# Gate matmuls in token groups inside a norm stage, in a one-core GNN and MoE kernel

## What is computed

```python
x = x + _L0_gnn_ref(_layernorm(x, axis=-1), ...)        # GIN layer: gather, two matmuls with batch norm
x = x + _L0_ffn_ref(_layernorm(x, axis=-1)[None], gate_w, experts)[0]
x = x + _L1_gnn_ref(_layernorm(x, axis=-1), ...)        # weighted gather, one matmul
x = x + _L1_ffn_ref(_layernorm(x, axis=-1)[None], ...)[0]   # 8 leaves, 512 -> 2048 -> 512 each
```

```python
gates = jnp.einsum('bhnd,hde->bhne', x4, gate_w)        # 1250 x 512 times 512 x 8
t = jnp.log(jnp.clip(gates, EPS)) / TEMPERATURE
for 8 iterations:                                       # Sinkhorn
    t = t - logsumexp(t, axis=-2)                       # over tokens
    t = t - logsumexp(t, axis=-1)                       # over experts
vals, idx = top_k(exp(t) per expert, 1250 // 8)
gate_values = (vals > 0.5)
routed = xf[idx]; outputs = einsum('hmei,eio->hmeo', routed, experts) * gate_values
```

## Time and profile before

| | us |
|---|---|
| median of 3 runs | 2508.84 |
| lowest, highest | 2504.61, 2509.62 |
| the profiled execution | 2508.55 |
| span of its trace | 2506.8 |
| norm stage c, first transpose to last lo part | 401.32 to 428.07 |
| from there to the start of `plan` | 428.07 to 441.14 |
| Sinkhorn, thresholds and places | 441.14 to 495.82 |

### The profile page before, as it was taken

The page is one execution under the profiler, slowest core; times in us unless marked ns, Lnnn a source line. Parts: engine busy times, 40 slices in busy tenths (PEclk is TensorE's granted clock), DMA queues, the critical chain, the costliest instruction groups (busy, mean ns, idle before and its releaser), DMA issues. The chain is left out here.

```text
span 2506.8 us, 34028 instructions
## 1 busy us (share of the span) xinstructions
PE 2298.5 (92%) x13384; PEld 2224.4 (89%) x13384; DVE 1033.3 (41%) x1695; ACT 701.1 (28%) x1204; POOL 323.6 (13%) x310
## 2 busy tenths in 40 slices
PE   3888886387989999999999999999999999999996
PEld 3777886366869999999999999999999999999996
DVE  7993346536362424324242432424233242423422
ACT  1335223064232222222222222222222222222221
POOL 1452000012001011101101110111111011101101
PEclk9998997598989999999999999999999999999998
DMA  1000201151020102102010210201011020101001
GB/s 65 2 2 1 68 1 49 47 189 52 34 77 2 68 1 78 34 34 78 1 67 6 72 34 34 78 1 67 13 65 34 34 78 1 67 17 61 34 1 41
DMA packets 73339, 105.93 MB, mean 42 GB/s; under 512 B 7219, under 2 KB 42499, under 8 KB 73211
## 3 DMA queue, kind: packets, MB, share of 16 engines
q1 hardware_dynamic: 68731, 100.37, 11.6%
q0 software_dynamic: 4480, 3.64, 0.5%
HBM read 95.08 MB, written 10.40 MB: 42 GB/s over the span
## 5 line engine op out<-in xcount | busy, mean ns | idle before, releaser
L1528 DVE TENSOR_TENSOR hidden_lo<-gelu,hidden_hi 128x416 fp32r<-128x416 f32 (+1 forms) x384 | 247.8, 645 | 1133.6 <-ACT hidden_hi L1596 1133.6
L1592 ACT ACTIVATE gelu<-psum,b1cols 128x416 f32<-128x416 f32 (+1 forms) x384 | 233.8, 609 | 1234.6 <-PE psum L475 1234.5
L473 PE MATMUL psum<-f_xT_hi,w_hi 128*128 128x416 f32 (+1 forms) x1536 | 543.2, 354 | 0.2 <-ACTq L1584 0.2
L473 PE MATMUL psum<-hidden_hi,w_hi 128*128 128x416 f32 (+1 forms) x1536 | 541.8, 353 | 1.4 <-DVE leaf_factors L1554 1.4
L474 PE MATMUL psum<-f_xT_lo,w_hi 128*128 128x416 f32 (+1 forms) x1536 | 542.0, 353 | 0.0
L475 PE MATMUL psum<-hidden_hi,w_lo 128*128 128x416 f32 (+1 forms) x1536 | 541.7, 353 | 0.0
L475 PE MATMUL psum<-f_xT_hi,w_lo 128*128 128x416 f32 (+1 forms) x1536 | 541.5, 353 | 0.0
L474 PE MATMUL psum<-hidden_lo,w_hi 128*128 128x416 f32 (+1 forms) x1536 | 539.2, 351 | 0.0
L1575 POOL TENSOR_TENSOR acc<-acc,y_scaled 128x416 f32<-128x416 f32 (+1 forms) x192 | 198.9, 1068 | 1544.8 <-DVE y_scaled L1519 1544.8
L473 PEld LDWEIGHTS psum<-f_xT_hi,w_hi 128*128 128x128 f32 x1536 | 290.1, 189 | 4.8 <-issue 1.9
L475 PEld LDWEIGHTS psum<-f_xT_hi,w_lo 128*128 128x128 f32 x1536 | 290.1, 189 | 4.2
(11 more groups left out here) (275 smaller groups left out, 1992.3 us busy)
## 6 DMA issues: line engine op xcount, KB each, us to landing
w_raw<-in_w SPq DMA_DIRECT2D x128, 512.0 KB, 4.1
expert_raw<-in_experts SPq DMA_DIRECT2D x8, 1024.0 KB, 5.8
leaf_all<-leaf_rows SPq DMA_DIRECT2D x8, 625.0 KB, 3.7
rows_by_place_d<-zero_rows SPq DMA_DIRECT2D x1, 2560.0 KB, 15.9
rows_by_place<-rows_by_place_d SPq DMA_DIRECT2D x5, 512.0 KB, 7.7
expert_results_d<-expert_results SPq DMA_DIRECT2D x16, 160.0 KB, 4.9
x_rows<-in_x SPq DMA_DIRECT2D x1, 2500.0 KB
out_rows<-x_rows SPq DMA_DIRECT2D x10, 250.0 KB
```

The costliest lines, as they stand in the source:

```text
L473: t.matmul(out, stat[0], mov[0], start=start, stop=False)
L1528: v.tensor_tensor(hlo[:, s % 4, 0:w], G[:, s % 3, 0:w], hhi[:, s % 4, 0:w].bitcast(F32), ALU.subtract).then_inc(lo_cut, 1)
L1592: a.activation(G[:, s % 3, 0:w], g.psum[:, 4 + s % 4, 0:w], ACT.Gelu, bias=g.b1cols[:, bass.ds(e * 16 + half * 8 + 2 * q + j, 1)]).then_in ...
```

## The change

A function `add_norm_gate` takes the place of `add_norm_turn` for this stage, and the gate part leaves `phase_route`.

```diff
+def add_norm_gate(nc, sem, g, produce, rows, thi, tlo):
+    LAG = 3
+    GROUPS = [(0, 4), (4, 8), (8, NT)]
...
+    def cols(i):
+        return g.psum[:, 4 + i % 3, 0:KD * TR].rearrange("p (k c) -> p k c", k=KD)
...
+        @block.sync
+        def _(sp):
+            for e in range(2):
+                sp.dma_start(g.eraw[:, e], g.experts[e].rearrange("(k p) d -> p k d", p=128)).then_inc(
+                    g.w_loaded[e], 16)
...
+        @block.vector
...
+            s.mark(v.memset(ghi[:, :, :].bitcast(F32), 0.0))
+            s.mark(v.memset(glo[:, :, :].bitcast(F32), 0.0))
+            s.wait()
+            s.then(v.tensor_copy(ghi[:, :, 0:NE], g.gate[:, :, :]))
+            v.tensor_tensor(glo[:, :, 0:NE], g.gate[:, :, :], ghi[:, :, 0:NE].bitcast(F32),
+                            ALU.subtract).then_inc(gate_cut, 1)
...
+        @block.scalar
...
+                if i < NT:
+                    deviation(a, g, stats, i)
+                if i in (8, 12):
+                    copy_gates((i - 8) // 4)
+            copy_gates(2)
...
+        @block.tensor
+        def _(t):
+            def gates(n):
+                lo, hi = GROUPS[n][0] * TR, GROUPS[n][1] * TR
+                t.wait_ge(lo_cut, GROUPS[n][1])
+                if n:
+                    t.wait_ge(gates_copied, n)
+                else:
+                    t.wait_ge(gate_cut, 1)
+                for k in range(KD):
+                    ins = cut_products(t, g.psum[:, 3, 0:hi - lo], (ghi[:, k, :], glo[:, k, :]),
+                                       (thi[:, k, lo:hi], tlo[:, k, lo:hi]), k == 0, k == KD - 1)
+                ins.then_inc(gated, 1)
...
+            for i in range(NT + LAG):
+                if i < NT:
+                    if i >= 3:
+                        t.wait_ge(added, i - 2)
+                    produce(t, i, g.psum[0:TR, i % 3, :]).then_inc(produced, 1)
+                j = i - LAG
+                if j >= 0:
+                    t.wait_ge(normed, j + 1)
+                    if j >= 3:
+                        t.wait_ge(lo_cut, j - 2)
...
+                    ins.then_inc(turned, 1)
+                if i == 8:
+                    gates(0)
+                if i == 11:
+                    turn_gates(0)
+                    gates(1)
+            turn_gates(1)
+            gates(2)
+            turn_gates(2).then_inc(g.gates_turned, 1)
```

More of the change, by code:

```diff
@@ L46 @@
 CH = PLACES // 2
+GATE_BANK = 7
 NG = NP // 128
@@ L873, in phase_route @@
     room = Room(nc, g.route_at)
-    gT = room("gates_T", [NE, N], F32)
     P16 = room("plan_sixteen_times", [TR, NT, NE, 16], F32)
@@ L878, in phase_route @@
     room = Room(nc, g.route_at2)
-    ghi = room("gate_hi", [128, KD, 128], F32R)
-    glo = room("gate_lo", [128, KD, 128], F32R)
     zero_rows = room("zero_rows", [128, D], F32)
@@ L900, in phase_route @@
     at = Record()
-    gated = sem("r_gated")
-    copied = sem("r_copied")
-    turned = sem("r_turned")
     to_sum = sem("r_to_sum")
@@ L922, in _ @@
             s = g.steps.on(v)
[L923 to L931, removed]
+            s.mark(v.memset(bits[:, :], 0))
+            v.wait_ge(g.gates_turned, 1)
+            s.then(v.tensor_scalar(plan[:, :, :], g.psum[0:TR, GATE_BANK, 0:NT * NE].rearrange(
+                "p (t e) -> p t e", t=NT), FLOOR, None, ALU.max))
             for i in range(SINKHORN):
@@ L1007, in _ @@
         def _(t):
[L1008 to L1021, removed]
             for i in range(SINKHORN):
@@ L1047, in _ @@
             over_tokens(5, g.upto, active).then_inc(back, 1)
[L1049 to L1053, removed]
         @block.gpsimd
@@ L1066, in _ @@
         def _(sp):
-            for e in range(2):
-                sp.dma_start(g.eraw[:, e], g.experts[e].rearrange("(k p) d -> p k d", p=128)).then_inc(
-                    g.w_loaded[e], 16)
             sp.wait_ge(zeroed, 1)
@@ L1813, in gnn_ffn_kernel @@
         g.y_rows = room("expert_results", [CH, 4, D], F32)
+        room = Room(nc, places_at - 8192)
+        g.gT = room("gates_T", [NE, N], F32)
+        g.ghi = room("gate_hi", [128, KD, 128], F32R)
+        g.glo = room("gate_lo", [128, KD, 128], F32R)
+        assert room.next <= g.y_at
         room = Room(nc, sent_at)
@@ L1827, in gnn_ffn_kernel @@
         g.placed_zero = sem("placed_zero")
-        add_norm_turn(nc, sem, g, "c", turn_y(g), g.c_rows, g.cthi, g.ctlo)
+        g.gates_turned = sem("gates_turned")
+        add_norm_gate(nc, sem, g, turn_y(g), g.c_rows, g.cthi, g.ctlo)
         phase_route(nc, sem, g)
```

51 lines of the change are left out of this document (added).

## The result

The changed kernel takes 2511.62 us (median of 12 runs, 2509.63 to 2513.65), the kernel before 2508.91 (12 runs on the same chip). The ratio, which is worked out from the single runs and is not the quotient of the two medians (they differ by 2.71 us, 0.11%), is 1.0017, with a 95% interval of 1.0009 to 1.0025: some 4 us slower by the ratio, and within the 0.2% that the prediction called no change. The prediction had 2512.3, in a range of 2507 to 2516.8.

What follows compares the result with a forecast made beforehand. DVE's step was taken to pace the norm stage's end, with DVE and PE taking turns in Sinkhorn; 2508.55 - 0.8 (start of `plan`) + 4.5 (Sinkhorn's waits) = 2512.25, say 2512.3 us, range 2507 to 2516.8.

Steps and rivals of the forecast that it cites:

- the start of `plan`: End of the norm stage's chain: `plan` starts at 440.3 against 441.14 before, -0.8 us.
- Sinkhorn beside POOL: First Sinkhorn iteration: two DVE multiplications wait for POOL's cast (+0.6) and subtract (+3.9), sum +4.5 us.
- rival 3: Sinkhorn: POOL does not hold DVE, 2507.8 us, or 2504.1 with the high clock too; chance 0.11.
- Gate parts ahead of the stage: Before DVE's first add: two memsets, cast and subtract, of which only 0.4 us lies on the path, +0.4.
- gates(0): Twelve matmuls between tile 5's transposes and produce(9): 2.7 us at the high clock, DVE waits about +2.0.
- rival 2: Norm stage: clock low in all three gate groups, `plan` +3.5, total 2516.6 us; chance 0.14.
- c_rows of tile 9: From DVE taking tile 9 to the end of its `c_rows`: 5.8 us, against 5.1 before, to 428.7.
- gates(1): Ahead of tile 9's transposes on PE: 5.0 us at the low clock, transposes start at 433.7.
- rival 1: Gate groups: the clock stays high since they fill PE's gaps, total 2508.6 us; chance 0.12.
- The tail: From tile 9's transposes to gates(2) 3.0 us; then gates(2), copy, two transposes and engine meeting, `plan` at 440.3.
- gates(2): Twelve matmuls of 250 columns starting at 436.7: 1.4 to 2.5 us, taken as 2.2 with the latency.
- The claim that most of the gate work stood in series: Norm stage: two thirds of the gate work is in series with DVE's steps; 13 us behind the stage become about 6.5.

Runs made afterwards that it cites:

- b_pool_late: The kernel before with one wait more, POOL's cast held until the gates are turned, gate groups unmoved; 2511.68 us, ratio 1.0014 to the kernel before.
- x_psum_operand: The changed kernel with Sinkhorn's two reciprocals written to PSUM, so both multiplications have one SBUF input; 2505.02 us, ratio 0.9993 to the kernel before.
- x_pool_memset: The changed kernel with POOL's cast and subtract replaced by memsets of the same buffers, expert 0's weights left out; 2506.31 us, ratio 1.0002 to the kernel before.
- x_tile9_first: The changed kernel with gates(1) behind tile 9's transposes and gates(2) in its own bank ahead of the second turning; 2509.38 us, ratio 1.0005 to before.
- x_gates_end: The changed kernel with all three gate groups behind the norm stage's last transposes, each in its own PSUM bank; 2509.2 us, ratio 1.0011 to before.
- x_spread: Changed kernel with gates(0) in four pieces, gates(1) and gates(2) behind the last transposes, POOL's cast and subtract in the norm stage; 2504.5 us, ratio 0.998 to before.

## Why the prediction came out right, step by step

**Forecast and sum.** The time was right, 2511.62 for 2512.3. The two terms, by the profiled executions: Sinkhorn +4.59 for +4.5; the start of `plan` +0.05 for -0.8. The rest of the kernel gave back 2.1 us that no term had. The medians differ by 2.71, the ratio says 4.3 and the interval 2.3 to 6.3, and the sum of 4.64 fits the last two. That the time came within 0.7 us is in part luck: in the term for `plan` an error of 1.7 us to one side and one of 1.1 to the other partly cancelled, and the 2.1 us that the rest of the kernel gave back, for which no term stood, more than covered the 0.9 that was left.

**Sinkhorn beside POOL** is right in cause and size: 0.85 and 3.78 for 0.6 and 3.9. POOL's cast ended where it had been put (2.29 us after DVE's memset of the bits, for 2.32), but DVE came to the multiplication sooner, 1.29 us after it instead of 1.4 to 1.6, since `plan` started together with the memset; so the first wait was longer. The row it rested on had 512 elements a row, and rival 3 said that 80 might slip in; b_pool_late, x_psum_operand and x_pool_memset end that rival. The Trainium skill ("SBUF — State Buffer", "Who interferes with whom") limits its rule: a DVE instruction with at most one SBUF input does not contend with GpSimd, DVE's 2-port modes aside, and one with two does not contend with a GpSimd instruction that only writes SBUF. The runs agree on both: with one input in PSUM the multiplications took 0.24 us beside the subtract of 4.50, and beside memsets of 1.80 they took 0.24 too.

**Gate parts ahead of the stage.** First add at +1.52 instead of +1.22: +0.3 for +0.4.

**gates(0)** is the mis-sized term. It was costed at 2.7 us, the high clock, from a window of the kernel before that had 1.00. It took 4.18: the first matmul stood 0.57 ahead of the second, the next six were some 0.41 apart and the last five 0.226. So DVE idled 3.65 us before tile 9, for 2.0, nearer to the 4 that the prediction gave as the sign of rival 2, and took the tile at +23.3 instead of +21.6. The pace at either clock was right (0.417 and 0.227 had been worked out), and so was the bound of 5.0 within 0.2; what failed was to read the phase of the clock in one execution as a property of the place. It was high from 415.7 to 422.5 before, and low until 421.6 after.

**c_rows of tile 9** was done 5.5 us after that, for 5.8. **gates(1)** began 0.4 us later still, the first turning being ahead of it on PE, and took 5.17 us for 5.0, wholly at the low clock, as the forecast had it and against rival 1. In two of the three other profiles with this stage it took 5.16 and 5.17 as well, but in x_pool_memset 4.08, so the 5.0 is likely at this place and not fixed to it.

**The tail.** From the transposes of tile 9 to gates(2) 2.63 us for 3.0. **gates(2)** 1.65 for 2.2: it had the high clock, and its 250 columns are 0.115 us apart. From its end to `plan` it took 1.19 us, where copy, turning and meeting had been put at 1.40. These three gave back 1.1 us, so that the term was 0.85 too low and no more. Rival 2 (low in all three groups, 2516.6) would have needed gates(2) at the low clock too.

**Sums and readings that don't come out.** From the stated terms the chain gives 437.2 with the high clock in all groups (the prediction has 436.6) and 443.4 with the low one (it has 444.6), so rival 2 would be 2515.3. The 6.5 us "behind the stage" are counted from the transposes of tile 9; from the last lo part it was 3.17. The rings of three banks cost nothing, as forecast, but the margin of over 2 us at every step was 1.68 and 1.40 us at the transposes of tiles 8 and 9.

**The claim that most of the gate work stood in series** is borne out and was too mild: the stage grew by 9.95 us and the part behind it shrank by 9.90. x_tile9_first (DVE's 6.00 us of idle time became 0.62) and x_gates_end (hiding nothing was 0.7 to 1.6 us better, the clock's share taken off) say the same, the sizes being as uncertain as the clock.

## What to carry to other kernels

Work that fills an engine's gaps is hidden only up to the slack of the step that it is put into, here 0.75 us on PE in the profile of the kernel before: a group of 4 to 5 us placed ahead of the last tile costs nearly what it cost behind the stage. With three matmuls a step DVE idled 1.17 us before tile 9 where the whole group made it idle 3.65. When a wait goes, look at what else starts at the same event and was kept apart by that wait; a DVE instruction with two SBUF inputs can then meet a POOL instruction that reads SBUF, and the loss shows as a longer instruction, with no idle time beside it. Two remedies took it away here: move POOL's work to where DVE has no instruction with two SBUF inputs, or put one of the inputs in PSUM. Cutting POOL's instruction into pieces took 1.85 of the 4.63 us. And before an edit in such a stage is priced from one profile, look at a second profile of the same stage: here two of them differed by 1.9 us.

## What the hardware showed that I had not expected

- DVE's reduction and reciprocal beside POOL's subtract kept their 0.24 and 0.22 us, with their one input in SBUF (L1046 and L1047 in the changed kernel's timeline, above); only instructions with two SBUF inputs were held.
- The phase of the clock in the norm stage differs from kernel to kernel: it rose at 415.7 (before), 421.6 (after), 423.2 (x_tile9_first), 427.2 (x_gates_end) and 422.5 (x_spread), in stages whose starts lie within 2.9 us. It differs between executions of one and the same stage too: the next rise came at 435.2 in the changed kernel, behind gates(1), and at 429.9 in x_pool_memset, within it. It is worth up to 2.5 us for one group of twelve matmuls (5.17 against 2.7), more than most edits here, and I could not read it from the order of the work.
